# A graph network on one core: its load reordered, X's own products and the degrees moved to other PSUM banks

## The reference

```
# layer 0
deg = clip(sum(adj, 1) + 1, 1);  h = (adj @ X + X) / deg
out = relu([X, h] @ W + b);      out /= max(norm(out), 1e-12)
# layer 1
h = tanh([X, t] @ W1 + b1) @ W2 + b2;  XB = X @ B.T
out = h + adj @ XB - sum(adj, 1) * XB
# layer 2: only the last 100 neighbours of a row count, each 0.5 ** (its rank from the end)
w = mask * where(pos > 0, 0.5 ** (k - pos), 0);  out = w @ (X @ weight) + bias
# layer 3
out = logmap(adj @ expmap(x)) @ kernel + bias
x = layernorm(x + out)           # after each layer
```

## Time and profile before

| | us |
|---|---|
| median of 3 runs (lowest, highest) | 166.24 (165.58, 166.6) |
| the profiled execution, its own time | 165.22 |
| its span, first to last instruction | 163.3 |
| busy: TensorE, VectorE, ScalarE, GpSimd | 112.1, 101.6, 70.2, 55.8 |

### The profile page before, as it was taken

How to read it: one execution, slowest core, us unless ns; L and a number is a source line. 1 busy time by engine, 2 the same in 40 slices (tenths; PEclk the granted TensorE clock), 3 DMA queues, 4 the chain that set the end, 5 groups by cost and what they waited for, 6 DMA issues and landing times.

```text
span 163.3 us, 3084 instructions
## 1 busy us (share of the span) xinstructions
PE 112.1 (69%) x1228; PEld 64.5 (40%) x1244; DVE 101.6 (62%) x227; ACT 70.2 (43%) x119; POOL 55.8 (34%) x67
## 2 busy tenths in 40 slices
PE   0000277658799559999679699999989899992000
PEld 0000156657124313546333366595446644561000
DVE  0064993999853999993969313545303888538861
ACT  0030213603749668954589745141034310257440
POOL 0000040132920936652145303416203461723290
PEclk9999999985559999999999999999999999999555
DMA  3999999999999992000000000000000000000006
GB/s 78 259 290 260 357 303 305 343 345 300 303 342 342 254 283 66 0 4 2 0 4 0 0 4 0 0 4 0 0 4 0 0 0 2 0 4 0 0 0 129
DMA packets 13950, 18.73 MB, mean 115 GB/s; under 512 B 5360, under 2 KB 5488, under 8 KB 13936
## 3 DMA queue, kind: packets, MB, share of 16 engines
q1 hardware_dynamic: 7728, 9.74, 21.5%
q10 hardware_dynamic: 6208, 8.78, 19.0%
HBM read 18.00 MB, written 0.52 MB: 113 GB/s over the span
## 4 chain that ended last, share of the span: by engine, by line
PE 43%; DVE 28%; DMA 7%; issue 6%; POOL 5%; ACT 4%; ACTq 2%; POOLq 1%; DVEq 0%
PE psC L892 7%; DMA stage<-adj 7%; PE psN L892 7%; PE psS L892 7%; DVE AT L612 6%; DVE AT L613 6%; PE psS L944 3%; POOL root L325 3%; PE psC L926 3%; PE psH L936 2%; POOL nroot L344 2%; PE psC L979 2%; PE psH L1033 2%; PE psH L1034 2%; DVE X L697 1%
## 5 line engine op out<-in xcount | busy, mean ns | idle before, releaser
L445 ACT ACTIVATE WT<-psC 128x1024 int16<-128x1024 f32 x32 | 31.1, 1024 | 10.8 <-PE psC L984 10.7
L325 POOL TENSOR_TENSOR root<-var,power 128x4 f32<-128x4 f32 (+1 forms) x16 | 18.7, 1173 | 44.2 <-DVE var L692 18.3
L936 PE MATMUL psH<-AT,cb 128*32 128x256 bf16 (+3 forms) x96 | 5.9, 374 | 20.8 <-DVE AT L613 20.7
L892 PE MATMUL psS<-AT,XP 128*128 128x512 bf16 x72 | 19.0, 386 | 1.0 <-issue 0.6
L612 DVE STREAM_TRANSPOSE AT<-stage 128x1024 bf16<-128x1024 bf16 x10 | 13.2, 1316 | 10.2 <-DMA stage<-adj 10.2
L892 PE MATMUL psN<-AT,XP 128*128 128x512 bf16 x44 | 11.1, 379 | 3.9 <-DVE XP L618 3.6
L613 DVE STREAM_TRANSPOSE AT<-stage 128x1024 bf16<-128x1024 bf16 x10 | 12.8, 1278 | 0.0
L338 POOL TENSOR_TENSOR XB<-X,weights 128x256 f32<-128x256 f32 x12 | 10.0, 849 | 5.6 <-DVE X L697 5.6
L936 PEld LDWEIGHTS psH<-AT,cb 128*32 128x32 bf16 x96 | 2.3, 106 | 24.1 <-issue 20.7
L892 PEld LDWEIGHTS psS<-AT,XP 128*128 128x128 f16 x80 | 7.3, 99 | 10.5 <-issue 3.8
L979 PE MATMUL psC<-later,cb 32*32 32x512 bf16 x256 | 9.8, 426 | 1.6 <-ACT WT L445 1.1
(11 more groups left out here) (162 smaller groups left out, 226.4 us busy)
## 6 DMA issues: line engine op xcount, KB each, us to landing
stage<-adj SPq DMA_DIRECT2D x20, 256.0 KB, 14.7
stage<-adj ACTq DMA_DIRECT2D x20, 256.0 KB, 10.5
WT<-adj ACTq DMA_DIRECT2D x12, 256.0 KB, 12.8
WT<-adj SPq DMA_DIRECT2D x12, 256.0 KB, 16.2
out<-X SPq DMA_DIRECT2D x6, 64.0 KB, 1.9
weights<-weights_packed SPq DMA_DIRECT2D x1, 353.5 KB, 17.6
cb<-constants_packed SPq DMA_DIRECT2D x1, 264.2 KB, 11.7
X<-x SPq DMA_DIRECT2D x2, 128.0 KB, 7.3
```

The lines of the kernel that those rows point to most:

```text
L325: nc.gpsimd.tensor_tensor(root[:, e, 0:n], var[:, e, 0:n], power[:, 0:n, 0:NR], ALU.pow).then_inc(root_ready, 1)
L445: nc.scalar.activation(WT[:, e, tiles], psC[:, PAIRS * h:PAIRS * (h + 1)], ACT.Relu).then_inc(chain_taken, 1)
L892: ins = nc.tensor.matmul(sum_bank(l, e), XP[:, l % 2, c], matrix, start=(c == 0), stop=last)
L936: ins = nc.tensor.matmul(psH[QD * g:QD * (g + 1), cols], one, AT[:, NQ * g + k, e, cols], start=(k == 0), stop=(k == NR - 1))
```

## The change

The load: both queues issue two pieces of adj ahead of X (one before), and the constants move from SyncE's queue to ScalarE's, behind X. VectorE accordingly transposes pieces 0 and 1 ahead of the largest magnitude, and takes X's mean while GpSimd works on the maximum; piece 2 comes ahead of the second half of X's split.

The banks: own_part writes psN and psS in turn, and no longer psC, so the chain does not wait for it; chain(0) and chain(1) are written between the products of X. degrees(0) stays in psH; degrees(1) to degrees(3) go to psX, on columns of their own, with new waits on TensorE. VectorE takes degrees(0) earlier (ahead of piece 5), degrees(1) later (behind piece 10 and split1(0)). In chunk 3 degrees comes ahead of spread and transpose_x(1, 1) goes behind dense(0, 3). centre("W2", "K") moves ahead of take_degrees(3). On GpSimd diagonals(3) moves ahead of the two var_root, and residual(1, 2) and residual(1, 3) wait until chunk 3 has been split.

```diff
         def z_bank(e):
-            return (psN[:], psC[:, 1], psC[:, 2], psC[:, 3])[e]
+            return (psN[:], psS[:])[e % 2]
+
+        def deg_bank(e):
+            return psH if e == 0 else psX
@@ SyncE @@
             load_lower(0)
+            load_lower(1)
             for q in range(NQ // 2):
                 sp.dma_start(X[QD * q:QD * (q + 1)], xd[q]).then_inc(x_loaded, 16)
-            load_lower(1)
-            sp.dma_start(cb[:].bitcast(U16), cpack).then_inc(consts_loaded, 16)
+            load_lower(2)
             sp.dma_start(weights[:, 0:first], wpack[:, 0:first]).then_inc(own_weights_loaded, 16)
-            for m in range(2, NR):
-                load_lower(m)
+            load_lower(3)
@@ GpSimd @@
             weigh(3)
+            diagonals(3)
+            var_root(0, 2)
             l2_root(3)
-            var_root(0, 2)
             var_root(0, 3)
-            diagonals(3)
+            pool.wait_ge(parts_ready, parts_count(1, 3))
             residual(1, 2)
             residual(1, 3)
@@ ScalarE @@
             load_upper(0)
+            load_upper(1)
             for q in range(NQ // 2, NQ):
                 act.dma_start(X[QD * q:QD * (q + 1)], xd[q]).then_inc(x_loaded, 16)
-            for m in range(1, 6):
+            act.dma_start(cb[:].bitcast(U16), cpack).then_inc(consts_loaded, 16)
+            for m in range(2, 6):
                 load_upper(m)
...
             take_z(0)
+            take_step(0)
+            load_upper(9)
             take_xt(0, 2)
-            load_upper(9)
             take_z(1)
+            load_upper(10)
+            take_step(1)
             take_xt(0, 3)
-            load_upper(10)
+            load_upper(11)
             take_z(2)
             take_z(3)
-            load_upper(11)
-            take_step(0)
+            take_counts(1)
             load_upper(12)
-            take_step(1)
-            take_counts(1)
+            take_step(2)
             load_upper(13)
-            take_step(2)
@@ VectorE @@
             transposes(0)
+            transposes(1)
             dve.wait_ge(x_loaded, 16 * NQ)
             nc.vector.tensor_reduce(xs[:, 0:1], X[:].rearrange("p c f -> p (c f)"), AX_X, ALU.max,
...
-            transposes(1)
...
+            transposes(2)
             dve.wait_ge(high_ready, 1)
...
-            for m in range(2, 5):
-                transposes(m)
+            transposes(3)
+            transposes(4)
+            take_degrees(0)
+            transposes(5)
             dve.wait_ge(weights_loaded, 16)
...
-            transposes(5)
-            take_degrees(0)
             transposes(6)
...
             transposes(9)
-            take_degrees(1)
             variance0(0)
             transposes(10)
             split1(0)
+            take_degrees(1)
             add_own_part(1)
...
             activate0(2)
+            centre("W2", "K")
             take_degrees(3)
...
-            centre("W2", "K")
             normalise(0, 3)
@@ TensorE, sum_block, first block of a sum in layer 0, e >= 1 @@
                         pe.wait_ge(sum_taken, e)
+                        pe.wait_ge(z_taken, NE)
@@ TensorE, transpose_x @@
+                if l == 1 and e < 2:
+                    pe.wait_ge(deg_taken, NE - 1 + e)
@@ TensorE, own_part @@
                 pe.wait_ge(xt_taken, e + 1)
+                if e % 2 == 1:
+                    pe.wait_ge(sum_taken, 1)
+                if e >= 2:
+                    pe.wait_ge(z_taken, e - 1)
@@ TensorE, degrees @@
-                pe.wait_ge(spread_taken, e + 1)
+                pe.wait_ge(spread_taken, 1) if e == 0 else pe.wait_ge(counts_taken, e + 1)
+                if e >= 2:
+                    pe.wait_ge(deg_taken, e)
@@ TensorE, chain @@
-                if i == 0:
-                    pe.wait_ge(z_taken, NE)
@@ TensorE, dense @@
                 if l == 0:
-                    pe.wait_ge(deg_taken, e + 1)
+                    pe.wait_ge(spread_taken, e + 1)
                     if e == 0:
+                        pe.wait_ge(deg_taken, 1)
@@ TensorE, the order at the program's end @@
             degrees(0)
+            chain(0)
             transpose_x(0, 2)
             own_part(1)
             dense(0, 0)
+            chain(1)
             transpose_x(0, 3)
             own_part(2)
             own_part(3)
-            chain(0)
-            chain(1)
...
                     if c == 5:
                         spread(e)
-                    if c == 9:
+                        degrees(e)
+                    if c == 11:
                         chain(NR * e - 1)
-                        degrees(e)
...
-            transpose_x(1, 1)
+            degrees(e)
             spread(e)
             sums(1, 0, range(1, 2))
-            degrees(e)
             chain(10)
             dense(0, e)
+            transpose_x(1, 1)
             hidden(1)
```

14 lines of the change are left out of this document (8 added, 6 removed).

## The result

| | before | after |
|---|---|---|
| median of 4 runs (lowest, highest) | 166.36 us (165.58, 166.6) | 161.15 us (160.72, 161.91) |
| the profiled execution; its span | 165.22; 163.3 | 161.91; 160.0 |
| busy: TensorE, VectorE, ScalarE, GpSimd | 112.1, 101.6, 70.2, 55.8 | 112.4, 100.2, 69.4, 55.7 |

The ratio is 0.972 (95% interval 0.965 to 0.979). The prediction said 162.1 us, with 160.2 to 164.8 as its range. Of the 4.15 us that it worked out the two profiles show 3.3, the medians 5.2.

A forecast was written before the change was run, and what follows sets the result against it. VectorE's 4.28 us wait for degrees(1) was taken as the bound. Front 2.85 plus layer 0's end 1.3 makes 4.15 us off the profiled 165.22, so 161.1; with 1.0 up to the median, 162.1 us, range 160.2 to 164.8.

The forecast's parts named there:

- What bounds the kernel: VectorE's 4.28 us wait for degrees(1) ahead of piece 10, not the load; towards layer 0's end the bound changes.
- The late X: Start: piece 1 ahead of X, maximum over partitions taken as 4.0 us; costs the first chunk 2.0 to 3.5, taken 2.7.
- the prediction's short end: Start, with a short maximum over partitions: piece 2's data at about 20 us decides, and X's split ends at 23.7.
- degrees(0) ahead of piece 5: VectorE's front: degrees(0) at 31.8 us, VectorE waits 1 us, piece 6 can start at 35.7, a loss of 1.0 us.
- ScalarE's queue: 264 KB more and later issue may delay pieces 6 and 7; piece 10 starts between 48.7 and 50.4, taken 49.7.
- ScalarE's half catches up: Rival on the load: piece 7 starts at VectorE's own 38.7, piece 10 at 48.7; 5.15 us won, 161.1; chance 0.2.
- The chain off the banks, degrees(1) behind piece 10: Before piece 10: the 4.28 us wait goes; add_own_part(1)'s new 0.7 us wait and the split's 0.7 us gain cancel.
- Sum of the front: Piece 10 starts at 49.7 for 52.55, 2.85 us earlier; piece 15 and TensorE's chunk 2 move along.
- The end of layer 0: TensorE's 1.31 us wait at 91.45 for the last chunk's split goes, ScalarE is next; 0.3 to 1.5 us, taken 1.3.
- The front is lost: Rival: late X and ScalarE's queue cost more, piece 10 starts at 52, only 1.9 us won, 164.3 to 165; chance 0.14.
- slower: Rival: ScalarE's later issue lands piece 10's upper half past 53.9; with 3 us more, 168 us; chance 0.05.
- Won in full: Rival: short maximum, ScalarE's halves catch up, piece 10 starts with its data at 47.6; 6.2 us won, 160.0; chance 0.12.

The follow-up runs named there:

- e9: Kernel before with only the constants moved from SyncE's queue to ScalarE's, behind piece 1; X stays behind piece 0: 161.9 us, ratio 0.984.
- e8: Changed kernel with take_degrees(1) put back ahead of variance0(0) and piece 10, all else as changed: 158.28 us, ratio 0.963.
- e6: Kernel before with 14 idle products on TensorE filling its stand between own_part(1) and dense(0, 0): 162.9 us, ratio 0.988.
- e1: Kernel before with the new load alone: two pieces ahead of X, constants on ScalarE's queue, VectorE's start to match: 161.98 us, ratio 0.989.
- e5: Changed kernel, not edited, run again beside the kernel before on another chip than the first group: 158.76 us, ratio 0.964.
- e3: Kernel before with centre and GpSimd's order and wait at layer 0's end as in the change, TensorE untouched: 164.99 us, ratio 1.015.
- e11: Kernel before with the new load and VectorE's and GpSimd's edits at layer 0's end; banks, chain and degrees as before: 162.31 us, ratio 0.984.
- e12: Changed kernel with centre and GpSimd's order and wait as before, TensorE's order at the end as changed: 159.25 us, ratio 0.968.
- e2: Changed kernel with the load, centre and GpSimd's order and wait as before; banks, chain, degrees and TensorE's end order stay: 162.28 us, ratio 0.984.

## Why the prediction was right, and where not

**What bounds the kernel: right.** VectorE stood for degrees(1), and what moved piece 10 moved the rest, except for 0.8 us ahead of piece 11 and the clock, both below.

**The late X: dearer by half than it came.** X landed as taken (VectorE began on it at 14.68; 15 predicted). The maximum over the partitions was the mis-sized term: GpSimd began it at 16.13 and its result was used at 17.15, directly behind X's mean, so it took at most 1.0 us, where 4.0 were taken. The row's 0.38 us was the nearer end, and the use 4.03 us on the earlier trace rows showed what VectorE did meanwhile, not the maximum. The parts were used at 23.29, 1.9 us later than before for the 2.7 predicted (24.1) and just under the bounds of 2.0 to 3.5. What decided instead is the prediction's short end: VectorE waited 1.75 us for the data of piece 2, began on it at 19.62 (about 20 predicted), and the split ended at 23.2 (23.7).

**degrees(0) ahead of piece 5: right, in part by luck.** Written at 31.82 (31.8), a wait of 1.98 us (1 predicted) and piece 6 at 35.45 (35.7). The 31.8 was 24.1 and 7.7 us of TensorE; it came as 23.29 and 8.53. TensorE did save its 0.8 us of waiting for piece 3, but its products behind the stand of 5.70 us ran slowly for longer and took that back.

**ScalarE's queue: the rival was right.** Piece 7 began at 38.47, VectorE's own time (38.7), and piece 10 at 48.14, below the 48.7 of "ScalarE's half catches up" and 1.6 below the 49.7 taken. No transfer held VectorE between pieces 6 and 9; piece 10's data did, for 0.48 us. The Trainium skill (DMA: Bandwidth & Descriptors, Issuing engines are not separate DMA queues) leads to that rival, and in this trace piece 7 agrees with it. But e9 shows that it doesn't follow that the choice of the queue is free: with one transfer of 264 KB moved, VectorE began on two pieces 1 to 2 us later and the kernel ran 3.2 us quicker (2.7 by the ratio), by way of TensorE's stand and its clock. The change of queue was priced as a cost with no gain of its own, and this is the prediction's largest blind spot: alone it gave half of what the whole change gave.

**The chain off the banks, degrees(1) behind piece 10: effect right, credit partly wrong.** The 4.28 us went, the wait of add_own_part(1) is 0.73 (0.7) and the split 0.42 for 1.16, so the two cancel as said. One term was left out: taking the 0.5 us of reading the degrees from ahead of piece 10 makes piece 10 earlier, but piece 11 has to pay it. And degrees(1) was ready at 46.7, 3 us earlier than the 49.8 reckoned, and e8 shows that its new place does nothing. What brought degrees(1) forward is that TensorE no longer stands and chain(0) no longer comes after the products of X; in e6, where only the stand is filled, it was read 1.74 us earlier and the kernel gained 1.9 to 2.4. In e1's profile the load alone had the wait gone as well, so the banks are one way to remove it and not the only one. The prediction listed the fallen clock among the facts of the profile and did not ask what it would be worth if the stand went.

**Sum of the front: 4.4 at piece 10 for 2.85 predicted, then a part lost.** "And so does piece 15" left out the 0.5 us of the degrees: of the 4.4, 3.58 were left at piece 11. "TensorE's work for chunk 2 starts with piece 11, hence moves along" is the step that failed in the first profile. Counts(2) did move, by 3.58 us, but ran into a clock of 0.50 to 0.58 from 56 to 59 us behind a wait of 1.40, and the chunk took 12.96 us for 11.12. In e5 this didn't happen, and the front was won by 4.79 us (65.93 for 70.72). Piece 15 started at 67.10 (67.6 predicted).

**The end of layer 0: size right, cause in part wrong.** 1.46 us were won for 1.3 predicted, and the late block started at 87.64 (87.3). The prediction added this up mainly from VectorE's and GpSimd's edits. They alone, e3 and e11, take 0.98 us off this stretch in the traces and nothing that the times can tell; without them, e12 and e2, the whole 1.46 us are there. So TensorE's own order (degrees(3) first, transpose_x(1, 1) behind dense(0, 3)) is enough, and the two sets of edits do not add up. On top of it the other edits take 0.5 us off the wait at the late block, and ScalarE takes it back one step on: it was named as next, with a wait of 0.76, and it is 0.49 now.

**The rivals.** "The front is lost" and "slower" needed a piece 10 at 52 or later, and nothing of it appeared. "Won in full" had piece 10 at 47.6 and 6.2 us won: e5 has piece 10 at 46.64, and against the kernel before of its own group it won 5.9 us by the ratio and 6.5 by the medians. So in the later runs this rival was nearer than the forecast of 4.15, and 158.8 lies outside the range (part of that is the kernel before itself, 165.29 there for the 166.24 that the range was built on). That the first comparison fell into the range owes something to errors against each other: the front under-rated by 1.6 us at piece 10 and 0.7 at piece 11, the clock in chunk 2 left out at 1.8.

**Two remedies for one wait.** By the medians the load alone gives 3.1 us (e1), the banks with TensorE's end 2.8 (e2), the rest 0.1 (e3); all together give 6.5 (e5; 5.2 in the first comparison). The sum holds nearly, but not because the parts are independent. With the new load on the old banks the stand shrank to 0.80 us in e1's profile and to 1.61 in e11's, and in the latter the clock fell and the wait was back. With the new banks there is work in the stand whatever the load does. In e1's profile, where the stand was short, counts(3) began at 66.08, 0.15 us behind e5's: there the banks would have brought nothing at the front, and the 1.4 us between the two spans (158.6 and 157.2) are the end of layer 0, 23.16 for 21.71. So the banks seem to be worth their gain only in executions in which the stand is long enough for the clock to fall. That this is why the parts add up is argued from single profiles, not shown. Open as well is why the constants' place delays piece 3 in e9; the queues' order was not traced packet by packet.
